# A pre-norm transformer on one core: input loads moved into the first norm's block, and the norm's Exp placed behind its Ln

## The chip, the cores and the metric

The kernel runs on one core of a Trainium2 chip. The metric is the device time of one launch in microseconds (us), lower is better. The core has five engines that run their own instruction queues and meet only through semaphores: TensorE (PE, matrix multiplies into PSUM; PEld is its weight load), VectorE (DVE), ScalarE (ACT, table-driven functions), GpSimd (POOL), and SyncE (SP), which here issues all DMA transfers and does the semaphore bookkeeping.

## The reference

The input `x` has 16 sequences of 256 tokens with 128 features. Four sublayers follow one another, each with its own layer norm in front and a residual around it:

```python
def _layernorm(x, axis=-1, eps=1e-05):
    m = jnp.mean(x, axis=axis, keepdims=True)
    v = jnp.var(x, axis=axis, keepdims=True)
    return (x - m) / jnp.sqrt(v + eps)
...
x = x + attention(_layernorm(x), ...)        # 16 heads of 8, causal
x = x + experts(_layernorm(x), ...)          # 8 experts, top 2, a gate per sequence
x = x + retention(_layernorm(x), ...)        # 4 heads, decay, gated output
x = x + window_layers(_layernorm(x), ...)    # 6 layers: local attention and a gated MLP
```

The four `_layernorm` calls in these lines are what the change touches. All data is float32.

## The kernel before

The stream `xT` lies in SBUF with the 128 features on the partitions and the 16 x 256 = 4096 tokens beside one another. The program is a chain of blocks. Each block gives every engine its own list of instructions and ends with a barrier of all engines, so no instruction of a block starts before all instructions of the block ahead have ended. The order is: a first block that loads inputs, `layer_norm` 0, `head_attention`, `layer_norm` 1, `experts`, `layer_norm` 2, `retention`, `layer_norm` 3, a small copying block, `layers` (six layers, the long part), and a block that adds and stores.

**The first block** (lines 135 to 162). SP issues 27 DMA transfers on one queue: `x` in four quarters of 512 KB, 19 weights and tables, and the four weights of the first window layer. All but the last four count on one semaphore, `loaded`. Behind them SP raises 108 semaphores by one each (the list `COUNTED`) and one more by eight. Later waits are written as `passed(n)`, which is n + 1, so these raised values are needed by every later block. Last, SP waits for `loaded`. Beside that DVE clears the padding of `xT` and sets `mean_w` (a matrix of 1/128) and `eps_col`.

**A norm** (`layer_norm`, lines 208 to 262) works on eight chunks of 512 tokens, chunk c in PSUM bank c:

- PE multiplies `xT` by `mean_w`, which gives the mean in all partitions (L232).
- DVE subtracts it and writes `norm` (L242).
- POOL squares `norm` into `logv` (L253).
- PE multiplies the squares by `mean_w`, which gives the variance (L229), two chunks behind the means.
- ACT takes Ln of variance plus epsilon into `logv` (L259), then Exp of -0.5 times that (L262), which is the inverse deviation.
- DVE multiplies `norm` by it in place (L247).

In the code ACT does all eight Ln first and then all eight Exp, and DVE does all eight subtractions first and then all eight multiplications. ACT evaluates functions from a table set. Where the program doesn't ask for a set, the compiler puts an `ACT_TABLE_LOAD` ahead of the first function that the active set lacks. `head_attention` asks for a set that has both Ln and Exp, `natural_log_exp_and_others`.

Of the kernel before, what the change touches and what calls it, by code (L numbers as in the profile page):

```python
# [16 lines left out]
ALU = mybir.AluOpType  # L17
# [3 lines left out]
P = 128  # L21
B, T, D = 16, 256, 128
PAD = 40
# [44 lines left out]
def passed(count):  # L68
    return count + 1
# [10 lines left out]
def program(nc, h, out):  # L80
# [48 lines left out]
    m_w2 = sb("m_w2", [MC, MG, P])  # L129
    m_col = sb("m_col", [P, 3 + 2 * MG])  # L130

    loaded = sem("loaded")
    n_loads = [0]

    with nc.Block() as block:
        @block.sync
        def _(sp):
            def load(dst, src):
                sp.dma_start(dst, src).then_inc(loaded, 16)
                n_loads[0] += 1  # L140
            for b in range(0, B, 4):
                load(xT[:, b:b + 4, PAD:], h["x"][:, b:b + 4, :])
            for dst, name in ((ident, "ident"), (a_w, "a_w"), (a_hm, "a_hm"), (a_mask, "a_mask"),
                              (e_wr, "e_wr"), (e_a, "e_a"), (e_b, "e_b"), (e_spread, "e_spread"),
                              (r_w, "r_w"), (r_wv, "r_wv"), (r_wg, "r_wg"), (r_wo, "r_wo"),
                              (r_tab, "r_tab"), (r_hm, "r_hm"), (r_decay, "r_decay"), (w_base, "w_base"),
                              (w_mask, "w_mask")):
                load(dst[:], h[name])
            load(e_before[:], h["e_before"].partition_broadcast(B))
            load(r_gn[:], h["r_gn"].partition_broadcast(P))  # L150
            load_window_weights(sp, sem("w_weights"), h, 0, w_qk, w_v, w_o, w_scl)
            for name in COUNTED:
                sp.sem_inc(sem(name), 1)
            sp.sem_inc(sem("m_residual"), NCH)
            sp.wait_ge(loaded, 16 * n_loads[0])

        @block.vector
        def _(dve):
            nc.vector.memset(xT[:, :, 0:PAD], 0.0)
            nc.vector.memset(xT[:, B, PAD:], 0.0)  # L160
            nc.vector.memset(mean_w[:], 1.0 / D)
            nc.vector.memset(eps_col[:], EPS)

    layer_norm(nc, sem, 0, xT, norm, logv, mean_w, eps_col, banks)
    head_attention(nc, sem, xT, norm, banks, ident, a_w, a_hm, a_mask)
    layer_norm(nc, sem, 1, xT, norm, logv, mean_w, eps_col, banks)
    experts(nc, sem, xT, norm, banks, ident, e_wr, e_a, e_b, e_spread, e_before)
# [37 lines left out]
            sp.wait_ge(stored, 16 * (B // PER))  # L205


def layer_norm(nc, sem, turn, xT, norm, logv, mean_w, eps_col, banks):

    mean_in, centred = sem("ln_mean"), sem("ln_centred")  # L210
    squared, var_in, logged = sem("ln_squared"), sem("ln_var"), sem("ln_logged")
    inverse, scaled = sem("ln_inverse"), sem("ln_scaled")
    done = NCH * turn

    def chunk(buf, c):
        return buf[:, c * CH:(c + 1) * CH]

    def of(buf):
        return buf.rearrange("p (b t) -> p b t", b=PER)

    def stream(c):
        return xT[:, c * PER:(c + 1) * PER, PAD:PAD + T]

    with nc.Block() as block:
        @block.tensor
        def _(pe):
            def variance(c):
                pe.wait_ge(squared, passed(done + c + 1))
                nc.tensor.matmul(banks[:, c, :], mean_w[:], chunk(logv, c), start=True, stop=True).then_inc(var_in, 1)  # L229

            for c in range(NCH):
                nc.tensor.matmul(of(banks[:, c, :]), mean_w[:], stream(c), start=True, stop=True).then_inc(mean_in, 1)  # L232
                if c >= BEHIND:
                    variance(c - BEHIND)
            for c in range(NCH - BEHIND, NCH):
                variance(c)

        @block.vector
        def _(dve):
            for c in range(NCH):  # L240
                dve.wait_ge(mean_in, passed(done + c + 1))
                nc.vector.tensor_tensor(of(chunk(norm, c)), stream(c), of(banks[:, c, :]), ALU.subtract)\  # L242
                    .then_inc(centred, 1)
            dve.wait_ge(centred, passed(done + NCH))
            for c in range(NCH):
                dve.wait_ge(inverse, passed(done + c + 1))
                nc.vector.tensor_tensor(chunk(norm, c), chunk(norm, c), chunk(logv, c), ALU.mult).then_inc(scaled, 1)  # L247

        @block.gpsimd
        def _(pool):  # L250
            for c in range(NCH):
                pool.wait_ge(centred, passed(done + c + 1))
                nc.gpsimd.tensor_tensor(chunk(logv, c), chunk(norm, c), chunk(norm, c), ALU.mult).then_inc(squared, 1)  # L253

        @block.scalar
        def _(act):
            for c in range(NCH):
                act.wait_ge(var_in, passed(done + c + 1))
                nc.scalar.activation(chunk(logv, c), banks[:, c, :], ACT.Ln, bias=eps_col[:]).then_inc(logged, 1)  # L259
            act.wait_ge(logged, passed(done + NCH))  # L260
            for c in range(NCH):
                nc.scalar.activation(chunk(logv, c), chunk(logv, c), ACT.Exp, scale=-0.5).then_inc(inverse, 1)  # L262


# [1328 lines left out]
```

## Time and profile before

| | |
|---|---|
| three timed runs | 3974.85, 3982.18, 3982.12 us, median 3982.12 us |
| the profiled execution | 3985.08 us, span 3983.3 us from the first to the last instruction |
| mean granted TensorE clock | 0.986 of 2.4 GHz |
| PE busy | 3795.3 us, 95% of the span |
| DVE, ACT, POOL busy | 3124.4, 2950.9, 2521.3 us |
| DMA | 27.95 MB, 7 GB/s over the span |

The span is divided by the blocks' barriers. The first block runs from 0 to 21.9 us, the four norms start at 21.9, 356.3, 424.4 and 637.6 us and take some 20 to 25 us each, and `layers` runs from 667 to 3975 us. Busy shares over the whole span are therefore the shares of `layers`; what a norm costs has to be read from its own stretch of the timeline. A timeline row gives the start, the time until the last of the row's instructions ended, the engine and line, the tile written and the tiles read, the count, and in brackets how long the engine was idle just before and whose work ended that.

### The profile page before, as it was taken

To read this page: it belongs to the slowest core of one execution; us is meant where nothing else is said; L and a number is where in the kernel's file an instruction comes from. 1 tells how busy PE (TensorE), PEld (TensorE's weight loads), DVE (VectorE), ACT (ScalarE), POOL (GpSimd) and SP (SyncE) were. 2 spreads that over 40 slices of the span, in tenths; PEclk is the share of its full clock that TensorE was granted. 3 is DMA by queue.
4 is the path that set the end of the run, shared out by engine and by line. 5 is a ranking of instruction groups with operands and counts; after the bars stand their busy time and mean duration, and the time that the engine had idled before them with its cause. 6 is when DMAs were issued, how large, how long until landed. Compare 5 with 4: busy or idle time off the path is not lost. (4 is left out here: it accounts for less than half of the span.)

```text
span 3983.3 us, 155012 instructions
## 1 busy us (share of the span) xinstructions
PE 3795.3 (95%) x61323; PEld 2391.7 (60%) x61339; DVE 3124.4 (78%) x4956; ACT 2950.9 (74%) x6593; POOL 2521.3 (63%) x2418
## 2 busy tenths in 40 slices
PE   6997797999999999999999999999999999999998
PEld 3665584666655666646666556666466665566663
DVE  4886565899957999848999669998489996699984
ACT  5985214888876888868888768888688887688885
POOL 3553233788845888717888448887178884488870
PEclk8999998999999999999999999999999999999999
DMA  2000000000000000000000000000000000000001
GB/s 76 1 0 1 0 0 1 1 0 5 0 23 2 0 5 0 1 23 1 0 5 0 23 2 0 5 0 1 23 1 0 5 0 23 2 0 5 0 1 43
DMA packets 12396, 27.95 MB, mean 7 GB/s; under 512 B 2460, under 2 KB 6728, under 8 KB 11344
## 3 DMA queue, kind: packets, MB, share of 16 engines
q1 hardware_dynamic: 12240, 25.72, 1.8%
q8 instruction: 116, 1.90, 0.2%
q14 instruction: 40, 0.33, 0.0%
HBM read 23.62 MB, written 2.10 MB: 6 GB/s over the span
## 5 line engine op out<-in xcount | busy, mean ns | idle before, releaser
L956 POOL TENSOR_TENSOR w_t<-w_t 128x512 f32<-128x512 f32 x768 | 979.2, 1285 | 519.9 <-DVE w_t L1259 519.9
L1259 DVE TENSOR_TENSOR w_t<-banks,w_tab 128x512 f32<-128x512 f32 x1536 | 955.5, 683 | 242.9 <-ACT w_sq L1396 234.2
L972 POOL TENSOR_TENSOR w_t<-w_t,w_rn 128x512 f32<-128x512 f32 x768 | 784.7, 1043 | 251.3 <-ACT w_rn L1445 251.3
L1052 PE MATMUL banks<-w_qk,w_xs 128*128 128x512 f32 x1536 | 825.5, 620 | 3.5 <-issue 2.4
L1072 PE MATMUL banks<-w_vo,w_xs 128*32 128x256 f32 x12288 | 823.0, 385 | 4.9 <-ACT w_us L1389 4.9
L1060 PEld LDWEIGHTS banks<-ident,w_t 128*128 128x128 f32 x3072 | 380.6, 140 | 426.8 <-issue 407.6
L1389 ACT ACTIVATE w_us<-banks 128x512 f32<-128x512 f32 x768 | 456.9, 595 | 161.0 <-PE banks L1072 156.2
L1060 PE MATMUL banks<-ident,w_t 128*128 128x128 f32 x3072 | 461.7, 273 | 19.1 <-POOL w_t L972 10.3
L1072 PEld LDWEIGHTS banks<-w_vo,w_xs 128*32 128x32 f32 x12288 | 321.8, 109 | 246.5 <-issue 81.3
L1296 DVE TENSOR_REDUCE w_ss<-w_sq 128x16 f32<-128x1024 f32 x384 | 464.2, 1209 | 0.0
L977 POOL TENSOR_TENSOR w_pr<-w_pr,w_rl 128x512 f32<-128x512 f32 x384 | 402.6, 1048 | 58.1 <-ACT w_rl L1450 58.1
L1111 PE MATMUL banks<-w_us,w_prT 128*32 128x128 f32 x10752 | 410.6, 273 | 15.6 <-issue 15.6
L1130 PEld LDWEIGHTS banks<-w_kT,w_qT 64*32 64x32 f32 x24576 | 319.6, 106 | 163.2 <-issue 163.2
L1111 PEld LDWEIGHTS banks<-w_us,w_prT 128*32 128x32 f32 x10752 | 349.4, 110 | 91.2 <-issue 29.1
L1130 PE MATMUL banks<-w_kT,w_qT 64*32 64x64 f32 x24576 | 381.5, 219 | 6.3 <-issue 6.3
L1396 ACT ACTIVATE w_sq<-banks 128x512 f32<-128x512 f32 x384 | 229.3, 597 | 181.2 <-PE banks L1052 172.5
L1277 DVE TENSOR_TENSOR w_pr<-banks,w_mx 128x256 f32<-128x256 f32 x768 | 289.6, 418 | 21.0
L1404 ACT ACTIVATE w_sq<-banks 128x512 f32<-128x512 f32 x384 | 230.3, 600 | 79.9 <-PE banks L1052 79.9
L1300 DVE TENSOR_REDUCE w_tot<-w_pr 128x8 f32<-128x512 f32 x384 | 263.1, 685 | 29.5 <-ACT w_pr L1419 10.3
L1052 PEld LDWEIGHTS banks<-w_qk,w_xs 128*128 128x128 f32 x1536 | 231.6, 190 | 91.1 <-issue 90.9
L1271 DVE TENSOR_REDUCE w_mx<-banks 128x8 f32<-128x512 f32 x384 | 265.5, 691 | 13.1
L1030 PE MATMUL banks<-logv,m_w 128*114 128x512 f32 x576 | 273.7, 610 | 0.0
(178 smaller groups left out, 5951.2 us busy)
## 6 DMA issues: line engine op xcount, KB each, us to landing
w_qk<-w_qk_in SPq DMA_DIRECT2D x7, 1024.0 KB, 4.8
w_v<-w_v_in SPq DMA_DIRECT2D x7, 512.0 KB, 5.5
w_o<-w_o_in SPq DMA_DIRECT2D x7, 512.0 KB, 6.3
m_w<-m_w_in SPq DMA_DIRECT2D x6, 342.0 KB
xT<-x_in SPq DMA_DIRECT2D x4, 512.0 KB
out<-kept SPq DMA_DIRECT2D x8, 256.0 KB, 2.4
m_w<-m_w_in SPq DMA_DIRECT2D x6, 171.0 KB
r_tab<-r_tab_in SPq DMA_DIRECT2D x1, 512.0 KB
```

Of the source, the lines that this page charges most:

```text
L956: nc.gpsimd.tensor_tensor(v1, v1, v2[:, :, ::-1, :], ALU.add).then_inc(S["added"], 1)
L972: nc.gpsimd.tensor_tensor(v1, v1, rn[j % 2][:, i * HALF:(i + 1) * HALF].unsqueeze(2) .broadcast_to([P, HALF, WD]), ALU.mult).then_inc(S["n ...
L977: nc.gpsimd.tensor_tensor(p[:], p[:], rl[j % 2][:].unsqueeze(1).unsqueeze(3) .broadcast_to([P, 2, HALF, WIN]), ALU.mult).then_inc(S["weigh ...
L1052: nc.tensor.matmul(banks[:, i, :], x[:], wqk[:, i * INNER + hh * C:i * INNER + (hh + 1) * C], start=True, stop=True).then_inc(S["qk"], 1)
L1060: last = nc.tensor.transpose(banks[:, 3 + i, g * P:(g + 1) * P], t1[j1 % 2][:, lo:lo + P], ident[:])
L1072: last = nc.tensor.matmul(banks[WIN * g:WIN * (g + 1), 2, lo:lo + 2 * P], x[:, WIN * w:WIN * (w + 1)], wvo[:, first:first + 2, :].rearrang ...
L1111: last = nc.tensor.matmul(banks[WIN * w:WIN * (w + 1), 7, 0:P], prT[:, chunk, WIN * w:WIN * (w + 1)], rhs, start=(hv == 0 and i == 0), sto ...
L1130: last = nc.tensor.matmul(bank[WIN * w:WIN * (w + 1), g], qT[j1 % 2][rows, g, WIN * w:WIN * (w + 1)], kT[rows, hk * NPAIR + g, lo:lo + 2 * ...
L1259: nc.vector.tensor_tensor(dst[j % 2][:, i * C:(i + 1) * C].rearrange("p (h d) -> p h d", d=WD), src, tab[:, 2 * t + cs, i * WD:(i + 1) * W ...
L1277: nc.vector.tensor_tensor(pr[j2 % 2][:, :, par * NPAIR:(par + 1) * NPAIR].rearrange("p a g r -> p g a r"), heads[:, par], mx[j2 % 2][:, pa ...
L1296: nc.vector.tensor_reduce(ss[j % 2][:], sq[:].rearrange("p a h d -> p (a h) d"), AX, ALU.add)\
L1389: nc.scalar.activation(us[j][:, 2 * a:2 * a + 2].rearrange("p w a n -> p (w a n)"), banks[:, 2, :], ACT.Copy).then_inc(S["u_taken"], 1)
```

## The change: where the loads stand, and the order of Ln, Exp and the multiplication

1. The 27 DMA issues and the wait for `loaded` move out of the first block into the block of `layer_norm` 0, as SP's part of it. SP's part of the first block is now only the 109 semaphore raises. Each quarter of `x` gets a semaphore of its own, and PE waits for quarter c // 2 ahead of the mean of chunk c.
2. In the first block DVE's four memsets stand in another order.
3. In all four norms ACT asks for `natural_log_exp_and_others` at the block's start, and the Exp of a chunk stands right behind its Ln.
4. In all four norms DVE multiplies chunk c - 4 right behind the subtraction of chunk c; the last four multiplications follow at the end.

```diff
+    def load_all(sp):
+        loaded = sem("loaded")
...
+        for i, b in enumerate(range(0, B, 4)):
+            sp.dma_start(xT[:, b:b + 4, PAD:], h["x"][:, b:b + 4, :]).then_inc(sem(f"x_loaded{i}"), 16)
...
+        load_window_weights(sp, sem("w_weights"), h, 0, w_qk, w_v, w_o, w_scl)
+        sp.wait_ge(loaded, 16 * n_loads[0])
 
     with nc.Block() as block:
         @block.sync
         def _(sp):
...
-            load_window_weights(sp, sem("w_weights"), h, 0, w_qk, w_v, w_o, w_scl)
             for name in COUNTED:
                 sp.sem_inc(sem(name), 1)
             sp.sem_inc(sem("m_residual"), NCH)
-            sp.wait_ge(loaded, 16 * n_loads[0])
...
-    layer_norm(nc, sem, 0, xT, norm, logv, mean_w, eps_col, banks)
+    layer_norm(nc, sem, 0, xT, norm, logv, mean_w, eps_col, banks, load_all)
...
+        if loads:
+            @block.sync
+            def _(sp):
+                loads(sp)
...
             for c in range(NCH):
+                if loads:
+                    pe.wait_ge(sem(f"x_loaded{c // 2}"), 16)
                 nc.tensor.matmul(of(banks[:, c, :]), mean_w[:], stream(c), start=True, stop=True).then_inc(mean_in, 1)
...
+            def scale(c):
+                dve.wait_ge(inverse, passed(done + c + 1))
+                dve.wait_ge(centred, passed(done + c + 1))
+                nc.vector.tensor_tensor(chunk(norm, c), chunk(norm, c), chunk(logv, c), ALU.mult).then_inc(scaled, 1)
...
-            dve.wait_ge(centred, passed(done + NCH))
-            for c in range(NCH):
-                dve.wait_ge(inverse, passed(done + c + 1))
-                nc.vector.tensor_tensor(chunk(norm, c), chunk(norm, c), chunk(logv, c), ALU.mult).then_inc(scaled, 1)
+                if c >= 2 * BEHIND:
+                    scale(c - 2 * BEHIND)
+            for c in range(NCH - 2 * BEHIND, NCH):
+                scale(c)
...
+            nc.scalar.preload_act_table_set("natural_log_exp_and_others")
             for c in range(NCH):
                 act.wait_ge(var_in, passed(done + c + 1))
                 nc.scalar.activation(chunk(logv, c), banks[:, c, :], ACT.Ln, bias=eps_col[:]).then_inc(logged, 1)
-            act.wait_ge(logged, passed(done + NCH))
-            for c in range(NCH):
+                act.wait_ge(logged, passed(done + c + 1))
                 nc.scalar.activation(chunk(logv, c), chunk(logv, c), ACT.Exp, scale=-0.5).then_inc(inverse, 1)
```

The list of ACT's instructions in the first norm, before (`x8` is eight of a kind in a row):

```order
L259 ACT_TABLE_LOAD
L259 ACTIVATE logv<-banks,eps_col 128x512 [waits ln_var] x8
L262 ACT_TABLE_LOAD
L262 ACTIVATE logv<-logv 128x512 [waits ln_logged]
L262 ACTIVATE logv<-logv 128x512 x7
```

The same place after the change, the table and the first of the eight pairs that follow (L275 is Ln, L277 is Exp; semaphore `ln_logged` is raised by the Ln):

```order
L272 ACT_TABLE_LOAD
L275 ACTIVATE logv<-banks,eps_col 128x512 [waits ln_var]
L277 ACTIVATE logv<-logv 128x512 [waits ln_logged]
...
L227 UNCONDITIONAL_BRANCH
L487 UNCONDITIONAL_BRANCH [waits barrier_Pool_Activation_PE_DVE_SP_release]
```

The second table load of this norm is gone, and each Exp waits for the Ln just ahead of it. In norms 1 and 2, which had no table load, L272 now stands as one.

DVE's instructions in the first norm, before:

```order
L242 TENSOR_TENSOR norm<-xT,banks 128x512 [waits ln_mean] x8
L247 TENSOR_TENSOR norm<-norm,logv 128x512 [waits ln_inverse,ln_centred]
L247 TENSOR_TENSOR norm<-norm,logv 128x512 [waits ln_inverse] x7
```

And after (L257 is the subtraction, L253 the multiplication of the chunk four behind):

```order
L257 TENSOR_TENSOR norm<-xT,banks 128x512 [waits ln_mean] x5
L253 TENSOR_TENSOR norm<-norm,logv 128x512 [waits ln_centred,ln_inverse]
...
L257 TENSOR_TENSOR norm<-xT,banks 128x512 [waits ln_mean]
L253 TENSOR_TENSOR norm<-norm,logv 128x512 [waits ln_centred,ln_inverse] x5
```

Four of the eight multiplications now stand behind one subtraction each, the last five in a row (the first of them belongs to the last subtraction).

## Rows read from the trace of the kernel before

**Rows 1.** Timeline of SP's queue in the first block.
```profile
0.75 2.10 SPq L139 DMA_DIRECT2D xT<-x_in  x4
...
12.71 0.43 SPq L1506 DMA_DIRECT2D w_qk<-w_qk_in  x1
...
14.14 0.43 SPq L1509 DMA_DIRECT2D w_scl<-w_scl_in  x1
```
**Rows 2.** Timeline, PE's start in the first norm.
```profile
21.96 5.46 PE L232 MATMUL banks<-xT,mean_w 128*128 128x512 f32 x6 [21.96 <-PEq L135]
```
**Rows 3.** Busy times by stretch of the first block; PE, PEld, DVE, ACT, POOL, clock, DMA share, GB/s.
```profile
0.00:4.30 4.30, 0.00 (x0) 0.00 (x0) 1.04 (x4) 0.00 (x0) 0.20 (x4) 1.00 0.45 118
0.00:19.90 19.90, 0.00 (x0) 0.00 (x0) 1.04 (x4) 0.00 (x0) 0.20 (x4) 1.00 0.93 320
```
**Rows 4.** DMA of 0 to 24 us: packets, MB, share; KB each, us to landing.
```profile
q1 hardware_dynamic: 5184, 7.47, 88.5%
...
w_qk<-w_qk_in SPq DMA_DIRECT2D x1, 1024.0 KB, 8.4
```
**Rows 5.** Page, DMA queues and issues: code fetches, and the stores at the end.
```profile
q8 instruction: 116, 1.90, 0.2%
...
out<-kept SPq DMA_DIRECT2D x8, 256.0 KB, 2.4
```
**Rows 6.** Timeline of norm 1: its first Ln and its last chunks.
```profile
360.51 0.69 ACT L259 ACTIVATE logv<-banks,eps_col 128x512 f32<-128x512 f32 x1 [6.22 <-PE banks L229]
...
368.24 0.69 DVE L242 TENSOR_TENSOR norm<-xT,banks 128x512 f32<-128x512 f32 x1 [1.03 <-PE banks L232]
369.00 1.04 POOL L253 TENSOR_TENSOR logv<-norm 128x512 f32<-128x512 f32 x1 [0.68 <-DVE norm L242]
369.10 0.69 ACT L259 ACTIVATE logv<-banks,eps_col 128x512 f32<-128x512 f32 x1 [1.03 <-PE banks L229]
...
370.10 1.12 PE L229 MATMUL banks<-logv,mean_w 128*128 128x512 f32 x2 [0.18 <-POOL logv L253]
371.26 0.69 ACT L259 ACTIVATE logv<-banks,eps_col 128x512 f32<-128x512 f32 x1 [0.62 <-PE banks L229]
371.98 4.27 ACT L262 ACTIVATE logv<-logv 128x512 f32<-128x512 f32 x8
372.71 4.90 DVE L247 TENSOR_TENSOR norm<-norm,logv 128x512 f32<-128x512 f32 x8 [3.79 <-ACT logv L262]
```
**Rows 7.** Timeline of the end of norm 0.
```profile
39.14 0.69 ACT L259 ACTIVATE logv<-banks,eps_col 128x512 f32<-128x512 f32 x1 [0.62 <-PE banks L229]
39.84 1.28 ACT L262 ACT_TABLE_LOAD   x1
...
41.87 4.90 DVE L247 TENSOR_TENSOR norm<-norm,logv 128x512 f32<-128x512 f32 x8 [5.07 <-ACT logv L262]
```
**Rows 8.** All instructions of line 262 (duration min/median/max, first and last start); waits of line 247.
```profile
L262 ACT ACTIVATE logv<-logv x32: 612/613/629, 41.1 to 659.8; 128x512 f32<-128x512 f32 x32
L262 ACT ACT_TABLE_LOAD  x2: 1283/1283/1283, 39.8 to 654.9; - x2
...
  ACT logv L262: 17.7, 4
```
**Rows 9.** Timeline, an Exp that waits for the Ln ahead of it, in `head_attention`.
```profile
231.65 0.46 ACT L493 ACTIVATE a_rtotal<-banks 128x256 f32<-128x256 f32 x1
232.14 0.42 ACT L495 ACTIVATE a_rtotal<-a_rtotal 128x256 f32<-128x256 f32 x1
```
**Rows 10.** POOL and DVE in `head_attention`: line 331 whole, then one meeting.
```profile
L331 POOL TENSOR_TENSOR a_sc<-a_sc,a_mx x64: 1543/1546/1548, 60.0 to 343.4; 128x512 f32<-128x512 f32 x64
...
104.25 0.69 DVE L451 TENSOR_TENSOR a_sc<-a_sc,a_mx 128x512 f32<-128x512 f32 x1
...
104.30 1.54 POOL L331 TENSOR_TENSOR a_sc<-a_sc,a_mx 128x512 f32<-128x512 f32 x1 [0.67 <-DVE a_mx L449]
```
**Rows 11.** Busy times of the stretch behind norm 0, same columns as rows 3.
```profile
47.00:65.00 18.00, 10.96 (x64) 7.03 (x65) 8.56 (x12) 7.30 (x14) 8.24 (x9) 0.50 0.00 0
```

More of the change, by code:

```diff
@@ L130, in program, with load @@
     m_col = sb("m_col", [P, 3 + 2 * MG])
-    loaded = sem("loaded")
-    n_loads = [0]
+    def load_all(sp):
+        loaded = sem("loaded")
+        n_loads = [0]
+        def load(dst, src):
+            sp.dma_start(dst, src).then_inc(loaded, 16)
+            n_loads[0] += 1
+        for i, b in enumerate(range(0, B, 4)):
+            sp.dma_start(xT[:, b:b + 4, PAD:], h["x"][:, b:b + 4, :]).then_inc(sem(f"x_loaded{i}"), 16)
+        for dst, name in ((ident, "ident"), (a_w, "a_w"), (a_hm, "a_hm"), (a_mask, "a_mask"),
+                          (e_wr, "e_wr"), (e_a, "e_a"), (e_b, "e_b"), (e_spread, "e_spread"),
+                          (r_w, "r_w"), (r_wv, "r_wv"), (r_wg, "r_wg"), (r_wo, "r_wo"),
+                          (r_tab, "r_tab"), (r_hm, "r_hm"), (r_decay, "r_decay"), (w_base, "w_base"),
+                          (w_mask, "w_mask")):
+            load(dst[:], h[name])
+        load(e_before[:], h["e_before"].partition_broadcast(B))
+        load(r_gn[:], h["r_gn"].partition_broadcast(P))
+        load_window_weights(sp, sem("w_weights"), h, 0, w_qk, w_v, w_o, w_scl)
+        sp.wait_ge(loaded, 16 * n_loads[0])
     with nc.Block() as block:
@@ L137, in _ @@
         def _(sp):
[L138 to L150, printed above, removed]
-            load_window_weights(sp, sem("w_weights"), h, 0, w_qk, w_v, w_o, w_scl)
             for name in COUNTED:
@@ L154, in _ @@
             sp.sem_inc(sem("m_residual"), NCH)
-            sp.wait_ge(loaded, 16 * n_loads[0])
         @block.vector
         def _(dve):
+            nc.vector.memset(mean_w[:], 1.0 / D)
+            nc.vector.memset(eps_col[:], EPS)
             nc.vector.memset(xT[:, :, 0:PAD], 0.0)
             nc.vector.memset(xT[:, B, PAD:], 0.0)
-            nc.vector.memset(mean_w[:], 1.0 / D)
-            nc.vector.memset(eps_col[:], EPS)
-    layer_norm(nc, sem, 0, xT, norm, logv, mean_w, eps_col, banks)
+    layer_norm(nc, sem, 0, xT, norm, logv, mean_w, eps_col, banks, load_all)
     head_attention(nc, sem, xT, norm, banks, ident, a_w, a_hm, a_mask)
@@ L205, in _, with layer_norm @@
             sp.wait_ge(stored, 16 * (B // PER))
-def layer_norm(nc, sem, turn, xT, norm, logv, mean_w, eps_col, banks):
+def layer_norm(nc, sem, turn, xT, norm, logv, mean_w, eps_col, banks, loads=None):
     mean_in, centred = sem("ln_mean"), sem("ln_centred")
```

## The prediction

> **What bounds the kernel now.** I read the page first: PE is busy for 95% of the span, but that is the six window layers, whose code the change leaves alone. What it touches is the stretch before 22 us and the four norms, each closed off by barriers, so time taken from the path of such a block comes off the whole. I therefore read the timeline of each block, then SP's queue and the DMA rate.
>
> In the first block no compute is waited for. DVE's four memsets, 1.04 us, are done before 4.3 us [rows 3]. SP issues its last transfer until 14.14 + 0.43 = 14.57 [rows 1], and PE starts at 21.96, released by the block's barrier [rows 2]. Which part of these 7.39 us is the 109 semaphore raises, and which the wait for the loads? At 19.9 us the queue had moved 320 GB/s x 19.9 us = 6.37 MB [rows 3]. That is the 7.47 MB of all loads [rows 4] less the last three transfers (512, 512 and 64 KB, 1.11 MB), so `w_qk`, the first one that doesn't count on `loaded`, was then moved; it landed at 12.71 + 8.4 = 21.1 [rows 1, 4], 1.2 us later. Its own 1.05 MB took 3.3 us at that mean rate, so what `loaded` counts was moved at 16.6 and in at about 18, and in any case before 21.1. That leaves the raises as what ends the block, 7.39 us or 68 ns each with the barrier in it.
>
> In a norm, the chunks follow one another every 0.69 + 1.03 = 1.72 us, and DVE waits for PE in each [rows 6]. That rate stays. The tail is what ACT sets: in norm 1 the last Ln ends at 371.95, then eight Exp take 4.27 us, and DVE's last multiplication ends at 372.71 + 4.90 = 377.61. DVE waits 3.79 us for the first Exp in norm 1, 5.07 in norm 0, and 17.7 over the four [rows 6 to 8], so norm 2 is like norm 1 and norm 3 like norm 0. The extra 1.28 us is the table load between Ln and Exp, which only norms 0 and 3 have [rows 7, 8].
>
> **The start.** SP's first block is now raises alone. They begin where `x` was issued, at 0.75, and the barrier lets go at 0.75 + 7.39 = 8.14. Then `x` is issued. Its first quarter, 0.524 MB, was moved at about 4.3 us before (118 GB/s x 4.3 = 0.51 MB [rows 3]), 3.55 us after the issue. `w_qk` took 1.2 us more to land; for half the size I take 1.0, so 4.55 in all. PE starts at 12.7 instead of 21.96: 9.3 us gained. Bounds for issue to landing: 2.4, the stores' row [rows 5], and 8.4, that of `w_qk` behind a full queue [rows 4], so a gain between 5.4 and 11.4. If the raises cost almost nothing and the 7.39 us are a wait after all, the gain is up to 16.
>
> The three other quarters come some 1.6 us apart (0.524 MB at 320 GB/s [rows 3]), and PE's first three means take 5.46 us, 1.8 each [rows 2]. Quarter 1 is due 3.6 us behind the first mean and lands after 1.6. The three added places where PE waits are covered, and nothing queues behind them; if a quarter came late, the variances behind it and then ACT would be late by the same.
>
> Behind the quarters all other loads are issued 7.39 us later than before. `loaded` is complete at about 18 + 7.4 = 25.4, at the latest 28.5. The norm's block, with this wait in it, ends near 46.77 - 9.3 - 5.0 = 32.5, so the loads are covered by 4 us or more; their first users stand behind that barrier.
>
> **The tails.** I work out norm 1. An Exp that waits for its Ln starts 0.03 us after it ends (231.65 + 0.46 = 232.11, next 232.14 [rows 9]). Two that don't wait overlap: eight Exp of 0.61 [rows 8] in 4.27 is a step of 0.52, so 0.09. The tail now starts at the Ln of chunk 5, 369.10 [rows 6]: Ln to 369.79, Exp 369.82 to 370.43, Ln of chunk 6 from 370.34, Exp 371.06 to 371.67. The last Ln could start at 371.58. It needs the variance, which was ready for 371.26 before.
>
> Here the change adds a collision. POOL's square of chunk 7 starts at 369.00. DVE's multiplication of chunk 3 now stands behind the subtraction that ends at 368.93, and its eight in 4.90 us are a step of 0.60, so it starts at about 368.85, just before POOL. A POOL instruction of the same size takes 1.04 us alone here [rows 6] and 1.54 in `head_attention`, where it starts 0.05 us after a DVE instruction that also reads two SBUF tiles [rows 10]. So I add 0.50 us to the square, and PE's last variance waits for it [rows 6]: the last Ln starts at 371.76, its Exp ends at 373.09. First Exp to first multiplication was 371.98 + 0.61 to 372.71, 0.12; the last multiplication runs 373.21 to 373.89. Norm 1 ends 3.72 us earlier. With no collision it is 3.90. If POOL also has to let the next multiplication by, its square starts at 370.13, ends 1.13 late, and 3.09 is left.
>
> This is where the Trainium skill speaks against the change ("SBUF — State Buffer", section "Who interferes with whom"): a VectorE instruction with two SBUF inputs and a GpSimd instruction that reads SBUF exclude each other, and whoever issues first blocks the other for its whole length. The trace agrees in kind with its half microsecond. By the rule taken hard, the second case, 3.09, is possible, and so is the turned order below.
>
> In the middle of a norm DVE has 0.69 + 0.68 us of work per 1.72 us, ACT 0.69 + 0.61, POOL 1.54: all fit. A square that is 0.5 us late is met by a variance that PE does two means later.
>
> Norms 0 and 3 gain 1.28 more, 5.00 each. The Trainium skill ("ScalarE: Activation LUTs", section "Table sets: the hidden batching unit") budgets some 2.7 us for every switch and says that one set holds both functions; the trace has 1.283 us for a load [rows 8], which is what counts. By the page's figure the two norms would give 2.8 us more in all. The loads added in norms 1 and 2 cost nothing: ACT is idle for 6.22 us ahead of its first Ln at 360.51 [rows 6], 4 of them within the block, which starts at 356.3. Without that cover it would be 1.28 each.
>
> Four tails: 2 x 3.72 + 2 x 5.00 = 17.4 us, with bounds 14.9 and 18.2.
>
> **The sum.** 9.3 + 17.4 = 26.7 us. The profiled execution, 3985.1 us, would be 3958.4. It lies 3.0 above the median of the runs, 3982.1, so the prediction is 3955.4 us. PE's clock I leave at zero: behind norm 0 it is granted half from 47 to 65 us [rows 11], where DVE and POOL are busy for under half of the time, so a stretch of half clock that shifts by a few us may give or cost up to 3 us.
>
> **The rivals.**
>
> *The wait was for the loads.* Then the raises are cheap, `x` is issued near 1 us, and the start gains 16 instead of 9.3: 3949 us. For it: nothing in the views shows a raise. Against: the byte count above. 8%.
>
> *The turned order.* POOL gets to SBUF first, DVE's multiplication waits for the whole square, and the next subtraction stands behind it. A chunk then takes 0.69 + 0.07 + 1.04 + 0.68 = 2.48 instead of 1.72, for four chunks: 3.0 us per norm, 12.2 in all, 3967.6 us. For it: the two would start within 0.15 us of one another. Against: the multiplication doesn't wait for a semaphore of the subtraction just ahead and POOL does. 11%.
>
> *The quarters land with the crowd.* `x` shares the queue with 5 MB more; if transfers are mixed, its first quarter is in only at about 26, the start loses 4, and the gain is the tails less that: 3969 us. Against: `w_qk`, between the others, landed on its own account at 21.1 while its successors were queued. 4%.
>
> *Slower.* ACT's and DVE's programs get more instructions ahead of the window loops, whose bodies move in the instruction memory, while the page counts 116 code fetches [rows 5]. The loops turn 14 times in each of six layers, 84 times. A new stall of 0.6 us in each is 50 us, and 3982.1 - 26.7 + 50 is 4006 us. It decides from 26.7 / 84 = 0.32 us per turn. For it only that the fetches exist; against, that 116 of them are 1.4 per turn for all five engines. 3%.
>
> *The forecast*, with a few us either way from the clock and from the landing: 74%, its own range 3949 to 3963: the bounds of start and tails give 3952.5 to 3961.8, the clock the rest.
>
> **The numbers.** A difference of 0.2%, 8 us, is about the least that a measurement of this kernel can tell from none; its three runs span 7.3 us. For that, and for the turned order and the early loads, the range is 3944 to 3968. Only the slower rival and an unfavourable mix of clock and late quarters lie within 8 us of before or above: faster 0.93, within 0.2% 0.04, slower 0.03.
>
> **What would show it.** PE's first matmul at 12 to 13 us, behind a wait for DMA. The last multiplication of norm 0 ending near 32.5 us, and in every norm the last multiplication ending 2.1 us after the last Ln starts, with one table load per norm. Squares of chunks 4 to 7 at 1.5 us, those of 0 to 3 at 1.04. No change in the length of `layers`. I am wrong if PE starts later than 16 us, if the chunks' step in a norm grows beyond 1.72 us, or if `layers` changes by more than 5 us.

## The result, and the profile after

| | before | after | predicted |
|---|---|---|---|
| median | 3981.57 us (4 runs, 3974.85 to 3982.18) | 3953.36 us (4 runs, 3951.95 to 3956.86) | 3955.4 (3944 to 3968) |
| ratio | 1 | 0.9930, 95% interval 0.9918 to 0.9942 | faster |
| profiled execution, span | 3985.08, 3983.3 | 3954.04, 3952.2 | |
| mean granted TensorE clock | 0.986 | 0.989 | |

The change is worth 28.2 us in the medians and 31.1 us in the two spans. A second build of the same kernel (e8 below) had 3957.59 us, so some 4 us of this can't be told from chance.

First the start. The two rows show how SP's queue and PE begin, in the timeline of after (start, time to the end of the last, engine, line, what; in brackets the idle time before and what ended it):

```profile
7.83 1.28 ACT L272 ACT_TABLE_LOAD   x1 [7.83 <-PEq L153]
7.83 2.10 SPq L141 DMA_DIRECT2D xT<-x_in  x4
...
12.42 4.84 PE L242 MATMUL banks<-xT,mean_w 128*128 128x512 f32 x6 [12.42 <-DMA xT<-x_in]
...
18.16 0.69 ACT L275 ACTIVATE logv<-banks,eps_col 128x512 f32<-128x512 f32 x1 [9.05 <-PE banks L237]
```

The barrier let go at 7.8 us, and PE's first matmul was released by the first quarter of `x`, 4.59 us after the issue. Before, it was at 21.96 behind the barrier [rows 2]. In the whole norm PE waited for `x` only this once, so the other quarters came in time. SP's waits (engine, line, what for: total us, times, longest) answer where the other loads went:

```profile
SPq L227 <- DMA r_gn<-r_gn_in: 4.2, 1, 4.2
```

SP's last issue ended at 21.01 + 0.43 = 21.44, so all that `loaded` counts was in at 25.6, 6 us ahead of the end of the norm's block.

Next the tail of norm 0, from the timeline of after. The same place before is in [rows 7], and with the same rhythm and no table load in [rows 6]:

```profile
25.89 0.69 DVE L257 TENSOR_TENSOR norm<-xT,banks 128x512 f32<-128x512 f32 x1 [0.43 <-PE banks L242]
26.49 3.56 DVE L253 TENSOR_TENSOR norm<-norm,logv 128x512 f32<-128x512 f32 x4
26.66 1.42 POOL L268 TENSOR_TENSOR logv<-norm 128x512 f32<-128x512 f32 x1 [0.30 <-DVE norm L257]
...
28.00 0.67 ACT L275 ACTIVATE logv<-banks,eps_col 128x512 f32<-128x512 f32 x1
28.13 1.13 PE L237 MATMUL banks<-logv,mean_w 128*128 128x512 f32 x2 [0.56 <-POOL logv L268]
28.70 0.63 ACT L277 ACTIVATE logv<-logv 128x512 f32<-128x512 f32 x1
29.29 0.69 ACT L275 ACTIVATE logv<-banks,eps_col 128x512 f32<-128x512 f32 x1
30.01 0.63 ACT L277 ACTIVATE logv<-logv 128x512 f32<-128x512 f32 x1
30.67 0.69 DVE L253 TENSOR_TENSOR norm<-norm,logv 128x512 f32<-128x512 f32 x1 [0.61 <-ACT logv L277]
```

From the start of the last subtraction to the end of the last multiplication it is 31.36 - 25.89 = 5.47 us. All four norms have this tail, within 0.01. Before, norms 1 and 2 had 377.61 - 368.24 = 9.37 [rows 6] and norms 0 and 3 had 10.66. The last Ln starts 1.22 us after the end of the last square, at 29.29, as it did before (norm 1: 370.04 to 371.26 [rows 6]), so it is still the square, by way of the variance, that sets it. But ACT is nearly as late by itself: it is at an Exp until 29.33, and at the distance of 0.54 us that the Ln at 28.00 keeps from the start of its Exp at 27.46, it could have started the last Ln at 29.24. So the late square costs some 0.05 us. The squares (minimum, median, maximum ns over all four norms) show the collision that was predicted:

```profile
L268 POOL TENSOR_TENSOR logv<-norm x32: 1038/1230/1422, 15.3 to 630.4; 128x512 f32<-128x512 f32 x32
...
L253 DVE TENSOR_TENSOR norm<-norm,logv x32: 677/684/1530, 21.3 to 634.4; 128x512 f32<-128x512 f32 x32
...
L272 ACT ACT_TABLE_LOAD  x4: 1283/1283/1283, 7.8 to 615.7; - x4
```

Chunks 0 to 3, beside which no multiplication runs, take 1.04, and chunks 4 to 7 take 1.42. The multiplications meet it too. The four in 3.56 us above show it: at the step of 0.60 that was seen before they would take 2.49. The one that starts while the last square runs waits for it and takes 1.53, as the longest of line 253, which is 0.85 of the difference; the rest is a wait for the Exp that ends at 29.33. The delay is over before ACT has the last Exp.

The table puts the span together. Each figure is a difference of two starts or ends in the timelines: PE's start in a norm, the end of its last multiplication, and the first instruction of `layers`.

| us | before | after | gain |
|---|---|---|---|
| PE's start in norm 0 | 21.96 | 12.42 | 9.54 |
| norm 0, first mean to last multiplication | 24.81 | 18.94 | 5.87 |
| norm 1 | 21.26 | 18.55 | 2.71 |
| norm 2 | 21.26 | 17.36 | 3.90 |
| norm 3 | 24.16 | 19.34 | 4.82 |
| all that lies between them, and the copy | 553.89 | 553.98 | -0.09 |
| `layers` to the end | 3315.93 | 3311.59 | 4.34 |
| span | 3983.3 | 3952.2 | 31.1 |

Norm 1 gained 1.2 us less than norm 2. PE's clock explains it. Busy times by stretch, with the granted clock in the third column from the end, are for after:

```profile
340.80:344.20 3.40, 3.34 (x4) 1.51 (x5) 0.69 (x1) 1.28 (x1) 0.49 (x1) 0.50 0.02 5
```

and for before, at the same place of norm 1:

```profile
356.30:360.50 4.20, 3.96 (x9) 1.73 (x10) 2.07 (x3) 0.00 (x0) 2.25 (x3) 1.00 0.01 4
```

At half clock (1.2 of 2.4 GHz) PE did 4 matmuls in the first 3.4 us. Before it did 9 in 4.2.

The row left over is `layers`. No instruction of it was changed, and it is 4.3 us shorter. Each trace is one execution, though. The profiled one of before took 3985.08 us, 3.5 us over its median, and in all groups of runs together the same program took from 3972.58 to 3986.14 us. The runs below were also used to find out what moves `layers`.

### The profile page after: what moved, and what is told of

Same layout as the page of the kernel before. It is cut to its first block and busy times, and to the rows that moved or that the text cites. A ratio compares the mean times of both kernels' runs of the same rounds, so it can differ in the third digit from the quotient of the medians.

```text
span 3952.2 us, 155056 instructions
## 1 busy us (share of the span) xinstructions
PE 3794.1 (96%) x61339; PEld 2390.2 (60%) x61339; DVE 3129.7 (79%) x4956; ACT 2953.3 (75%) x6593; POOL 2526.3 (64%) x2418
## 5 line engine op out<-in xcount | busy, mean ns | idle before, releaser
L971 POOL TENSOR_TENSOR w_t<-w_t 128x512 f32<-128x512 f32 x768 | 978.3, 1283 | 517.8 <-DVE w_t L1274 517.8
L1315 DVE TENSOR_REDUCE w_tot<-w_pr 128x8 f32<-128x512 f32 x384 | 263.3, 686 | 29.8 <-ACT w_pr L1434 10.5
```

What stands on the lines that cost most here:

```text
L971: nc.gpsimd.tensor_tensor(v1, v1, v2[:, :, ::-1, :], ALU.add).then_inc(S["added"], 1)
```

## The experiments

Kernels of one group shared the runs of before; its median stands in brackets. Parts of a diff that repeat the change itself are left out.

### e1 and e2: each half alone [before 3981.74]

e1 is before with the new first block and the loads in norm 0, the norms' order as it was. e2 is before with the new norms, the loads as they were.

```diff
 # e1: before plus parts 1 and 2 of the change
+    layer_norm(nc, sem, 0, xT, norm, logv, mean_w, eps_col, banks, load_all)
 # e2: before plus parts 3 and 4 of the change
+            nc.scalar.preload_act_table_set("natural_log_exp_and_others")
...
+                if c >= 2 * BEHIND:
+                    scale(c - 2 * BEHIND)
```

> Only the loads move into the first norm's block; Ln, Exp and multiplications stand as before. If start and tails are independent parts: PE's first matmul at 12.4 us as in the changed kernel, norm 0 ends at 46.8 - 9.5 = 37.2, and the kernel gains 9.5 us. Rival (most of the gain is elsewhere, such as in the clock of the window layers): the gain in the runs differs from 9.5 by more than 5 us while the stretch up to the end of norm 0 gains 9.5.

> Only the norms change; the loads stand in the first block as before. Theory: PE starts at 21.96, from the last subtraction to the last multiplication norms 0 and 3 take 5.5 us instead of 10.65, norms 1 and 2 5.5 instead of 9.37, together 18.1 us gained, of which up to 2 may come or go with the clock at a norm's start. If the collision on SBUF cost something, squares would be longer and the tails over 6 us.

e1: 3972.4 us, ratio 0.9974 (0.9963 to 0.9986); PE starts at 12.42, the tails stay at 10.67 and 9.38, `layers` 3316.5. e2: 3967.64 us, ratio 0.9961 (0.9947 to 0.9975); PE starts at 21.82, all tails are 5.48, `layers` 3318.0. The halves gain 9.3 and 14.1 us, 23.4 together, and act on places of their own. e2 was expected to gain 18.1. In its trace the four norms do give 17.4 us, but `layers` is 2.1 us longer than in before's. Neither half shortens `layers`.

### e3: what ended the first block [before 3981.74]

The 109 raises go from SP to POOL, which is idle there. The loads and their wait stay on SP as before.

```diff
-            for name in COUNTED:
-                sp.sem_inc(sem(name), 1)
-            sp.sem_inc(sem("m_residual"), NCH)
             sp.wait_ge(loaded, 16 * n_loads[0])
 
+        @block.gpsimd
+        def _(pool):
+            for name in COUNTED:
+                pool.sem_inc(sem(name), 1)
+            pool.sem_inc(sem("m_residual"), NCH)
```

> The kernel before, with the 109 semaphore raises on POOL instead of SP. If the raises end the first block, it now ends when the loads have landed, at 18 to 19 us, and PE starts at 18 to 19 instead of 21.96, 3 us earlier. If the first block waited for the loads, PE still starts at 21.96.

It took 3980.26 us, ratio 0.9995 (0.9986 to 1.0004), which in the whole is not to be told from before. Its trace tells what the total can't. The ends of the queues in the first block (behind the durations the start of the drain, with which a queue ends ahead of the barrier) and PE's start:

```profile
L135 POOLq DRAIN  x1: 41/41/41, 9.6 to 9.6; - x1
...
L135 SPq DRAIN  x1: 7/7/7, 19.2 to 19.2; - x1
...
19.52 5.27 PE L235 MATMUL banks<-xT,mean_w 128*128 128x512 f32 x6 [19.52 <-PEq L135]
```

SP issued its last transfer by 13.88 + 0.43 = 14.31 and now drains at 19.2: that is the wait for the loads. Before, it drained at 21.7. So the raises did end the block, but without them the wait for the loads ends it 2.44 us earlier (21.96 - 19.52) and no more. The predicted "in at about 18" was 19.1.

### e4, e7, e11: the raises beside the loads [before 3981.74, 3982.02, 3980.62]

From after: `x` is issued first in the first block, and the raises are spread over engines. e4 gives 36 each to PE, ACT and POOL (and POOL the one of `m_residual`), e7 gives 28 to SP behind the four issues, 42 to ACT, 38 to POOL and none to PE. e11 is e4 again.

```diff
-            for name in COUNTED:
-                sp.sem_inc(sem(name), 1)
-            sp.sem_inc(sem("m_residual"), NCH)
+            for i, b in enumerate(range(0, B, 4)):
+                sp.dma_start(xT[:, b:b + 4, PAD:], h["x"][:, b:b + 4, :]).then_inc(sem(f"x_loaded{i}"), 16)
 # e4: COUNTED[0::3] on PE, [1::3] on ACT, [2::3] on POOL
 # e7: COUNTED[0:28] on SP, [28:70] on ACT, [70:] on POOL
```

> The changed kernel, with the four quarters of x issued by SP in the first block and the 109 raises divided among PE, ACT and POOL, 36 or 37 each. Theory (a raise costs 60 to 68 ns of its queue): the first block ends at about 3.1 us, the first quarter lands 4.5 us after its issue at 0.75, and PE starts at 5.3 us instead of 12.4: 7.1 us less than the changed kernel, 3946 us. If the raises are cheap and the landing is slow, PE starts no earlier than some 10 us; if a raise costs more on PE, ACT or POOL than on SP, PE's start shows by how much. All loads land before norm 0 ends at about 24.3, but by 5 us only.

> As the kernel with x issued in the first block, but the 109 raises on SP behind the issues (28), ACT (42) and POOL (39), none on PE, where a raise took 151 ns against 59 on SP, 67 on ACT and 78 on POOL. The first block then ends at about 4.7 us and PE starts when the first quarter lands, at 5.1 instead of 6.63: 1.5 us less, 11 units of 0.14 at most. The runs should give 3940 us, and 3945 if the short window layers of the last profile, 3304.7 us, were chance.

> The kernel with x in the first block and a third of the raises on PE, unchanged. If its short layers belong to the program, they take 3304 to 3306 us again and the runs give 3941; if they were chance, 3308 to 3316 us and 3945 to 3950.

Where the queues of e4 end, and PE's start:

```profile
L151 SPq DRAIN  x1: 125/125/125, 2.9 to 2.9; - x1
L151 ACTq DRAIN  x1: 8/8/8, 3.2 to 3.2; - x1
L151 POOLq DRAIN  x1: 41/41/41, 3.6 to 3.6; - x1
L151 PEldq DRAIN  x1: 8/8/8, 6.3 to 6.3; - x1
...
6.63 5.46 PE L255 MATMUL banks<-xT,mean_w 128*128 128x512 f32 x6 [6.63 <-PEq L151]
```

In e4 PE's own 36 raises end the block; in e7, without them, PE starts at 5.24, released by the first quarter of `x`, 4.5 us after its issue again. e7 has 3947.43 us, ratio 0.9922 (0.9908 to 0.9935). It was expected at 3940, or at 3945 if e4's short `layers` was chance. But e4, expected at 3946, starts 1.4 us later and has 3941.26 us (0.9879 to 0.9909), e11 3940.25 (0.9883 to 0.9914). Where do these 6 to 7 us come from? `layers` is 3304.7 and 3302.4 in e4 and e11, and 3309.1 in e7. On PE the two differ by nothing but the 36 raises ahead of all its work.

### e5: the table set alone [before 3982.02]

```diff
+            nc.scalar.preload_act_table_set("natural_log_exp_and_others")
             for c in range(NCH):
```

> The kernel before with one line more: each norm asks for the set with Ln and Exp at its start; all Exp still follow all Ln. If the table load is a term of its own: the tails of norms 0 and 3 fall from 10.65 to 9.37 us, those of norms 1 and 2 stay at 9.37, and 2.6 us are gained in all; the loads now first in norms 1 and 2 are covered. If the order is what matters and the load would be hidden anyway, the tails stay as they are.

3978.49 us, ratio 0.9995 (0.9986 to 1.0004). The timeline of ACT at the end of norm 0, beside [rows 7]:

```profile
38.72 0.69 ACT L260 ACTIVATE logv<-banks,eps_col 128x512 f32<-128x512 f32 x1 [0.62 <-PE banks L229]
39.44 4.27 ACT L263 ACTIVATE logv<-logv 128x512 f32<-128x512 f32 x8
```

The 1.28 us between Ln and Exp are gone and all four tails are 9.38. That is the whole of what norms 0 and 3 have over the others, as the prediction had it, and it is too little to be seen in the total. In this trace `layers` takes 3309.6 us, 6.3 less than in before's, with three changes of layer at half clock instead of six (more on these below). One line on ACT isn't shown to be the cause of that: e5's median is only 3.5 us under before's, and the interval of the ratio includes 1.

### e6: the multiplications at the end again [before 3982.02]

From after, DVE's part of the norm as before; ACT's pairs stay.

```diff
-                if c >= 2 * BEHIND:
-                    scale(c - 2 * BEHIND)
-            for c in range(NCH - 2 * BEHIND, NCH):
-                scale(c)
+            dve.wait_ge(centred, passed(done + NCH))
+            for c in range(NCH):
+                dve.wait_ge(inverse, passed(done + c + 1))
+                nc.vector.tensor_tensor(chunk(norm, c), chunk(norm, c), chunk(logv, c), ALU.mult).then_inc(scaled, 1)
```

> The changed kernel with DVE's eight multiplications behind all eight subtractions, as before the change; ACT's pairs stay. If the two SBUF readers collide, squares of chunks 4 to 7 fall from 1.42 to 1.04 us. The tail stays at 5.5 us: eight multiplications in steps of 0.60 from 0.6 us after the last subtraction's start end 5.5 us after it, and ACT's last Exp comes as late. So the time is that of the changed kernel. If the early multiplications carry part of the gain, the tails get longer by up to 2.4 us (four steps of 0.60).

3957.42 us, ratio 0.9943 (0.9927 to 0.9959). I expected the tail to stay at 5.5; it is 6.47 in all four norms. The timeline of norm 0 in e6:

```profile
25.52 0.69 DVE L252 TENSOR_TENSOR norm<-xT,banks 128x512 f32<-128x512 f32 x1 [1.03 <-PE banks L242]
...
26.25 5.75 DVE L257 TENSOR_TENSOR norm<-norm,logv 128x512 f32<-128x512 f32 x8
26.29 1.54 POOL L263 TENSOR_TENSOR logv<-norm 128x512 f32<-128x512 f32 x1 [0.68 <-DVE norm L252]
```

The eight multiplications take 5.75 us. Before, the same eight took 4.90, with no square beside them [rows 6]. POOL's square starts 0.04 us behind DVE's first and takes 0.50 more than alone, and a multiplication behind waits for it, which is the 0.85: each engine waits for the other in turn. The squares of chunks 4 to 6, beside which no multiplication runs now, are back at 1.04 us, as was expected; that of chunk 7 is the one with 1.54, in all four norms. So the multiplications were what made the squares longer. With all eight multiplications left, DVE ends the tail, and the delay counts. The early multiplications are thus worth 0.99 us a norm, 0.85 of it by keeping this collision off the path, and Ln beside Exp the other 2.9 (norms 0 and 3 have the table load's 1.28 on top). These 4 us in the four norms don't show in the medians: e8, the changed kernel in the same group of runs, has 3957.59 us.

### e8 and e9, e10: 36 instructions on PE that do nothing [before 3982.02 for e8, 3980.62 for e9 and e10]

e8 is after, built again. e9 is after with 36 raises on PE in the first block, of a semaphore that nobody waits for. SP's 109 raises beside them take longer. e10 is e7 with the same 36 in the copying block behind the last norm, where PE has nothing to do.

```diff
+        @block.tensor
+        def _(pe):
+            for _ in range(36):
+                pe.sem_inc(sem("gate"), 1)
```

> The changed kernel unchanged, beside the others on the same chip. Start, norms and blocks between them should repeat within 0.1 us except where PE's clock is granted at another moment (norms' first chunks, up to 1.2 us). If the length of the window layers follows the time at half clock in them and not the code, it comes out anywhere from 3305 to 3318 us, near 3302 plus 0.6 to 0.9 us for each us at half clock there; if the change itself shortened the layers by 4.4 us, it repeats at 3311.6.

> The changed kernel with 36 raises of an unused semaphore on PE in the first block, 5.4 us beside SP's 6.9, so that PE's program is as much longer ahead of the window loops as in the kernel with x in the first block and a third of the raises on PE (window layers 3304.7 us, six joints of 96 to 97 us). If the place of PE's instructions sets the layers' length, they fall from 3311.6 to some 3305 us, the joints behind the last projection of a layer from 97.4 to 100 us to 96.5, and the kernel gains some 6 us on the changed one. If that was the clock of one execution or something else of that kernel, the layers stay at 3308 to 3314.

> The kernel with no raises on PE, and 36 raises of an unused semaphore on PE in the copying block behind the last norm, where PE has nothing to do for 5.5 us. If the place of PE's instructions sets the layers' length: PE starts at 5.2 as there, the layers take 3305 instead of 3309 us, and the runs give 3940 us. If not: 3947 us as without them.

| | median us | ratio, 95% | PE's start | `layers` |
|---|---|---|---|---|
| e8, after again | 3957.59 | 0.9930 to 0.9957 | 12.39 | 3311.6 |
| e9, after and 36 | 3945.1 | 0.9898 to 0.9925 | 12.28 | 3300.1 |
| e7, spread | 3947.43 | 0.9908 to 0.9935 | 5.24 | 3309.1 |
| e10, spread and 36 | 3937.99 | 0.9878 to 0.9909 | 5.23 | 3302.5 |

PE starts as before (0.14 us earlier at most), and still 6.6 to 11.5 us go out of `layers`. In the medians it is 9.4 us for e10 against e7, and for e9 8.3 against after's 3953.36 or 12.5 against e8 of another group. PE's groups over 667 to 3950 us show what changed (last columns: busy us, mean ns | idle us before, and what ended it). After:

```profile
L1067 PE MATMUL banks<-w_qk,w_xs 128*128 128x512 f32 x1524 | 817.0, 618 | 2.4 <-issue 2.4
...
L1126 PE MATMUL banks<-w_us,w_prT 128*32 128x128 f32 x10752 | 409.9, 273 | 15.6 <-issue 15.6
...
L1045 PE MATMUL banks<-logv,m_w 128*114 128x512 f32 x576 | 270.5, 604 | 0.0
```

and the same lines, five further down, in e9:

```profile
L1072 PE MATMUL banks<-w_qk,w_xs 128*128 128x512 f32 x1524 | 818.2, 619 | 12.9 <-issue 12.9
...
L1131 PE MATMUL banks<-w_us,w_prT 128*32 128x128 f32 x10752 | 409.8, 273 | 6.5 <-issue 6.5
...
L1050 PE MATMUL banks<-logv,m_w 128*114 128x512 f32 x576 | 265.5, 595 | 0.0
```

The idle time without a releaser isn't less: 9.1 us left one line and 10.5 came to another. It has moved from inside the change of layer, ahead of the last attention matmuls and the MLP, to its end, ahead of the first `w_qk` matmuls of the next layer. And the MLP's matmuls became faster by 9 ns in the mean, though nothing in them changed.

### e12: the same 36 in the kernel before [before 3980.09]

The diff to before is the one above.

> The kernel before with 36 raises on TensorE in its first block, of a semaphore that nobody waits for; nothing else is changed. They are done by about 6.5 us, and the block ends at 21.96, so they cost nothing by themselves. Theory: what shortens the six layers is where TensorE's instructions lie, whatever the norms and the loads look like. Before, TensorE idles with no releaser for 1.45 to 1.76 us ahead of L1111 at every change of layer (six times), and half clock follows there; with the 36 instructions more that wait is expected ahead of the L1052 matmuls instead, as in the two padded kernels, and `layers` is 3303 to 3308 us instead of 3315.9: a median some 8 to 12 us under before's, near 3972. Rival one: the padding works only together with the changed norms or the clock of their time; then `layers` stays at 3314 to 3318 and the median within 3 us of before's. Rival two: chance of the run; then `layers` lies anywhere between 3310 and 3320 and the wait ahead of L1111 is still there.

3970.86 us, ratio 0.9976 (0.9967 to 0.9985), and `layers` is 3301.8 instead of 3315.9. The norms, their tails and PE's start (21.64) are as before. So the effect needs nothing of the change: the first theory held. In the medians it is 9.2 us, not 14.1, since before's profiled execution lies 5.0 us over the median of this group and e12's on its own. PE in e12 ahead of the second layer:

```profile
1223.80 1.96 PE L1057 MATMUL banks<-w_qk,w_xs 128*128 128x512 f32 x4 [2.22 <-issue]
```

And at a change of layer in before, where e12 has no such row, with the clock behind it:

```profile
1138.30 0.86 PE L1111 MATMUL banks<-w_us,w_prT 128*32 128x128 f32 x22
1140.62 0.65 PE L1111 MATMUL banks<-w_us,w_prT 128*32 128x128 f32 x6 [1.45 <-issue]
1141.19 3.15 PE L1030 MATMUL banks<-logv,m_w 128*114 128x512 f32 x4
...
1140.20:1143.60 3.40, 2.98 (x9) 1.28 (x9) 0.42 (x2) 0.79 (x2) 0.00 (x0) 0.50 0.00 0
```

PE idles in the middle of line 1111, is granted half clock, and four MLP matmuls take 3.15 us instead of the 1.97 that they take in e9. Before has such a dip at all six changes of layer, after at four of them. In after's trace:

```profile
1115.60:1119.00 3.40, 3.40 (x9) 1.79 (x8) 0.88 (x2) 0.54 (x2) 0.00 (x0) 0.50 0.00 0
1665.20:1668.60 3.40, 3.40 (x42) 1.97 (x41) 0.88 (x2) 2.03 (x5) 1.07 (x2) 1.00 0.00 0
```

The first is a change of layer with the dip, 9 matmuls, the second one without it, 42 (of other shapes too). From a layer's last `w_qk` matmul to the first of the next it takes 99.1 to 100.0 us in after where the dip falls and 97.4 to 97.6 in the two where it doesn't. Those two gain 3.7 us over before (99.47 and 99.16 there), and the other three lose 1.5 of that. In e9, e10 and e12, where the idle time has gone from line 1111, it takes 96.4 to 97.0. The last change, which has no next layer, ends after 109.2 us in before and after, and 103.8 in the three. In e12 all six changes together are 17.8 us shorter than in before, and the loops between them are 3.6 us longer.

Which of the changes have the dip is a matter of the execution: e8, the same program as after, has it at three and not at four. All 14 traces together tell the clock from the idle time, since each has five changes with a next layer. With the idle time ahead of line 1111 (or the same line further down) and the dip, such a change takes 99.7 us in the mean (29 of them, 98.8 to 101.2); with the same idle time and no dip 97.7 (16, 97.4 to 98.1); with the idle time gone from there 96.7 (25, 96.3 to 97.3), and none of these has a dip. The last change takes 108.1 to 110.2, 106.0 to 106.6 and 103.5 to 104.0 us.

The page of each trace counts code fetches. It has 116 in all nine without the 36 instructions on PE and 122, one more for each layer, in all five with them (e4, e9 to e12). That of e12:

```profile
q8 instruction: 122, 2.00, 0.2%
```

The DMA view over 1138.0 to 1141.0 us of before, around the idle time above:

```profile
q8 instruction: 1, 0.02, 1.9%
```

And over 1219.0 to 1224.0 us of e12, around its 2.22 us:

```profile
q8 instruction: 2, 0.03, 4.9%
```

In both, PE falls idle within 0.2 us of the end of a fetch (1139.16 and 1139.25 us in before, 1221.59 and 1221.45 in e12).

e9, e10 and e12 gained more in `layers` than was expected of them: it took 3300.1 us in e9 and 3302.5 in e10 where 3305 was expected, and 3301.8 in e12 where the lower end was 3303.

## Why the prediction was right, and where it was off

The sum of the prediction was 26.7 us. Outside `layers` the spans differ by 31.1 - 4.3 = 26.8. That the two are within 0.1 is luck in part: the start gave 0.2 more and the tails 0.7 more than I had summed, PE's clock in the norms took 0.9 back.

- **What bounds the start.** Right: raises, then `x`. PE at 12.42 (12.7 forecast), a gain of 9.5. e3 shows that the raises did end the first block. The barrier let go at 7.83 instead of 8.14. The wait for loads was nearer behind it than I had it, 2.4 us and not 3.9. The rival that made the raises cheap is out.
- **Issue to landing**, taken as 4.55 us: 4.59 after, and 4.5 in e7. The quarters weren't held up by the 5 MB behind them, and no wait for one shows.
- **The loads behind the norm.** Forecast complete at 25.4, at the latest 28.5: 25.6.
- **The tails.** I took 3.72 us for norms 1 and 2 and 5.00 for 0 and 3; 3.90 and 5.18 were measured, the bound that I gave for no collision. That they meet it is luck, for the collision is there, 0.38 us in each late square instead of the 0.50 taken. I had DVE start 0.15 us ahead of POOL and used the price of a meeting with 0.05 us between them; it was 0.17. My chain put the last Ln 371.76 - 368.24 = 3.52 us behind the last subtraction, by the variance; with 0.38 it is 3.40, and 3.40 was measured (29.29 - 25.89), 0.05 us after ACT could have started it. From there to the end I had 2.13 and 2.07 was measured, which makes up for the 0.05. This step is mis-sized by 0.18 us a norm, 0.7 in all. That DVE would have to wait as well was not in my chain; it is hidden by ACT, and e6 shows its price where DVE ends the tail, 0.85 us.
- **The turned order.** It did not come: subtraction, multiplication and square follow each other in 1.72 us to the end (24.17 to 25.89, DVE's last two subtractions). But one multiplication a norm does stand behind the whole rest of a square, in the tail, and takes 1.53 us instead of 0.68. The Trainium skill ("SBUF — State Buffer", section "Who interferes with whom") has such mutual exclusion for the whole length of the instruction that came first. The trace agrees in both directions, with 0.38 and 0.50 us for POOL and 0.85 for DVE. Each of these is 0.14 us less than what was left of the other's instruction by the trace when the delayed one started (0.52, 0.65 and 0.98 us).
- **The table.** e5 confirms 1.28 us for norm 0 and for norm 3, and that the loads added to norms 1 and 2 are hidden: with the load in place ACT still idled 4.10 us ahead of its first Ln of norm 1, at 346.21. The 2.7 us that the Trainium skill budgets for a switch ("ScalarE: Activation LUTs", section "Table sets: the hidden batching unit") are not seen; 1283 ns is the measured length, each of four times.
- **The clock**, left at zero with 3 us either way: norm 1 lost 1.2 us to a start at half clock, norm 0 won some 0.7 in its first chunks, norm 3 lost 0.4. Four norms with no such luck would have given 18.2; they gave 17.3.
- **"No change in the length of `layers`".** The traces have 4.3 us less, within the bound of 5 us that was put on it, and 3311.6 in both builds. But this is not shown to come from the change. The nine traces without the 36 instructions on PE have 3309.1 to 3318.0 us, with three to six dips of the clock at changes of layer, the same program differs in its dips from one execution to the next, and before's profiled execution had all six and lay 3.5 us over its median. The medians gain 28.2 us, and 24.4 with e8's build in another group of runs, on either side of the 26.8 that start and norms give. So no gain of `layers` is needed to account for them; one of a few us isn't excluded either. What the prediction didn't have is how easily code that lies elsewhere moves this term. The rival "slower" had named the right kind of thing, but on ACT and DVE, in every one of 84 turns, and as a loss. The runs with the 36 instructions show it on PE, at six changes of layer, and as a gain of 8 to 12 us in the medians. The change itself adds waits for `x` to PE's code, but its trace keeps the idle times in the attention matmuls (line 1126 there) and the 116 fetches.

How far the clock and how far the idle time makes the 14.1 us between the traces of before and e12 can be estimated from the 14 traces. A change of layer takes 99.1 us in the mean in before, 97.7 with the same idle time and no dip, and 96.7 in e12; the last one 109.3, 106.3 and 103.8. That is some 10 us for the clock (five times 1.4, and 3.0) and some 8 for the idle time (five times 1.0, and 2.5). The loops between the changes give 3.6 back, and why they do is open. PE is at half clock in `layers` between 700 and 3950 us for 23.9 us in before and 6.8 in e12. The dips come behind such an idle time, but not behind each: after idles 1.73 us until 1663.62 and keeps its clock.

What makes PE idle there is open too. The code fetches speak for the loading of code: six more of them with the 36 instructions, and a fetch that ends where the idle time begins. But before has 99 fetches from 690 us on and only twelve idle times of over 0.8 us beside one, and no run changed the layers' own code, so this is argued and not shown.

The best version is e10, 3937.99 us: ratio 0.9894 to before, 15.4 us under after. Of the 16.1 us between their spans 7.2 are PE's earlier start and 9.1 are `layers`, and the second part hangs on all the code ahead of the loops.

## What to carry to other kernels

Where blocks are closed off by barriers, read each block's own end and not the shares of the whole: 7 us of semaphore raises and four tails of 4 to 5 us, 0.7% of the time, were invisible in the page and could be worked out to a microsecond. In a chain of Ln, Exp and multiplication per chunk, put each function right behind the other on ACT with one table set, and let the multiplications start early enough that DVE isn't the engine that ends the tail, since there a collision with POOL counts in full. And before 5 to 10 us of a long kernel are put down to an edit, look at the blocks that it doesn't touch, with a second execution and with a build that only shifts their code; and compare medians with medians, for one profiled execution can lie 5 us off its own.

## What the runs showed of the hardware

A raise of a semaphore isn't free, and costs differ by engine. From the drains above: SP's 109 raises go from 0.75 to 7.6 us in after, 63 ns each. On POOL in e3 it is (9.6 - 0.8) / 109 = 81 ns, on ACT in e4 (3.2 - 0.8) / 36 = 67, and on PE (6.3 - 0.8) / 36 = 153.

```profile
L153 SPq DRAIN  x1: 7/7/7, 7.6 to 7.6; - x1
```

Where PE idles for 1.5 to 2.3 us at each change of layer is worth 8 to 12 us in the medians (14 between the traces of before and e12), and 36 instructions in the first block, over 600 us ahead of the first layer, are enough to move it. What the half clock takes at a change of layer is some 2 us (99.7 against 97.7).
